# Two graph-attention layers on one core: a head group's value product as one block of matmuls or as four quarters

## What is computed

```python
h = jnp.maximum(_layernorm(x, axis=-1), 0.0)
# layer 0: 8 heads of 32 features
Q, K, V = (proj(Wq, bq), proj(Wk, bk), proj(Wv, bv))
scores = jnp.einsum('bhnd,bhmd->bhnm', Q, K) * SCALE
scores = jnp.where(adj[:, None, :, :] == 0, -jnp.inf, scores)
attn = jax.nn.softmax(scores, axis=-1)
out = jnp.einsum('bhnm,bhmd->bhnd', attn, V)      # the value product
x = x + (out.transpose(0, 2, 1, 3).reshape(b, n, DOUT) @ Wo.T + bo)
# layer 1: edge scores of relu(layernorm(x)), leaky relu, masked softmax, product with the features
```

## Time and profile before

| | |
|---|---|
| median of 3 runs (lowest to highest) | 3978.39 us (3978.27 to 3991.85) |
| span of the profiled execution, first to last instruction | 3976.3 us |
| mean granted TensorE clock over the span | 0.967 of full speed |
| busy share of TensorE matmul / weight load / VectorE / ScalarE / GpSimd | 92% / 73% / 79% / 57% / 17% |

### The profile page before, as it was taken

One profiled execution on the slowest core, in us unless ns is written; L12 is line 12 of the kernel. 1 busy time (PEld: TensorE's weight loads), 2 busy tenths in 40 slices (PEclk: granted clock), 3 DMA queues, 4 the chain that ended last, 5 costly groups with the idle time before them and its releaser, 6 DMA issues.

```text
span 3976.3 us, 94630 instructions
## 1 busy us (share of the span) xinstructions
PE 3669.7 (92%) x34096; PEld 2908.9 (73%) x34096; DVE 3128.6 (79%) x5926; ACT 2267.1 (57%) x3940; POOL 674.9 (17%) x440
## 2 busy tenths in 40 slices
PE   6989989899998989989899898998989989899998
PEld 5777777777777767777777777776777767777776
DVE  6968778687886978869788696886968869688785
ACT  3837547275573845738456384663836638366482
POOL 1021030310303103031020301203012030120300
PEclk8999999999999999999999999999999999999999
DMA  5041220403204032040310503104031040311300
GB/s 151 2 105 36 60 82 2 117 25 70 71 2 118 23 76 66 2 131 10 81 61 4 137 2 83 59 15 126 2 89 53 21 121 2 95 47 31 99 2 12
DMA packets 129070, 227.67 MB, mean 57 GB/s; under 512 B 20672, under 2 KB 71104, under 8 KB 128448
## 3 DMA queue, kind: packets, MB, share of 16 engines
q1 hardware_dynamic: 128448, 219.50, 20.3%
HBM read 101.98 MB, written 16.78 MB: 30 GB/s over the span
## 4 chain that ended last, share of the span: by engine, by line
PE 68%; SPq 11%; issue 9%; DVE 7%; DMA 2%; ACT 1%; DVEq 0%; POOL 0%; POOLq 0%; ACTq 0%
PE pT L856 21%; PE ps L837 15%; PE pO L873 13%; SPq L220 11%; PE ps L773 8%; PE pO L975 7%; PE pT L908 2%; DMA adj_half<-in_adj_dram 2%; PE pT L963 2%; DVE pt L525 1%; DVE most L483 1%; DVE sm L667 1%; PE pO L884 1%; DVE sm L510 1%; DVE sm L674 1%
## 5 line engine op out<-in xcount | busy, mean ns | idle before, releaser
L349 ACT ACTIVATE sm<-sm,mn 128x1024 f32<-128x1024 f32 x1024 | 1179.5, 1152 | 454.8 <-DVE mn L510 452.5
L510 DVE CUSTOM_DVE_ANT_0 sm<-ps,bias 128x1024 f32<-128x1024 f32 x1024 | 1250.9, 1223 | 197.5 <-PE ps L837 178.0
L856 PE MATMUL pT<-ident,sm 128*128 128x128 f32 x8192 | 1098.6, 276 | 40.3 <-DVE pt L525 37.1
L856 PEld LDWEIGHTS pT<-ident,sm 128*128 128x128 f32 x8192 | 961.3, 142 | 218.5 <-DVE pt L525 52.8
L837 PE MATMUL ps<-ks,qs 96*128 96x512 f32 x2048 | 754.4, 451 | 4.6 <-issue 3.7
L525 DVE COPY pt<-pT 128x512 f32<-128x512 f32 x1024 | 702.4, 686 | 31.5 <-PE pT L856 30.8
L873 PE MATMUL pO<-pt,v 128*32 128x128 f32 x16384 | 649.7, 278 | 4.8 <-DVE pt L525 4.8
L359 ACT COPY pt<-pT 128x512 f32<-128x512 f32 x1024 | 583.2, 570 | 56.7 <-PE pT L856 56.4
L290 POOL TENSOR_SCALAR bias<-adj_half 128x512 bf16<-128x512 int32 x240 | 468.0, 1950 | 864.3 <-DMA adj_half<-in_adj_dram 855.7
L873 PEld LDWEIGHTS pO<-pt,v 128*32 128x32 f32 x16384 | 388.2, 109 | 170.1 <-issue 170.1
L975 PE MATMUL pO<-h,pt 128*128 128x256 f32 x2048 | 463.0, 379 | 0.0
(11 more groups left out here) (104 smaller groups left out, 3526.5 us busy)
## 6 DMA issues: line engine op xcount, KB each, us to landing
adj_half<-in_adj_dram SPq DMA_DIRECT2D x256, 256.0 KB, 2.8
ks<-pt SPq DMA_DIRECT2D x384, 128.0 KB, 2.4
qs<-pt SPq DMA_DIRECT2D x384, 128.0 KB, 2.4
xf<-in_x_dram SPq DMA_DIRECT2D x16, 1024.0 KB, 8.0
x<-in_x_dram SPq DMA_DIRECT2D x16, 1024.0 KB, 5.7
out_dram<-x SPq DMA_DIRECT2D x128, 128.0 KB, 2.9
x<-in_L_gnn_Wq_dram SPq DMA_DIRECT2D x1, 256.0 KB, 2.8
x<-in_L_gnn_Wk_dram SPq DMA_DIRECT2D x1, 256.0 KB, 3.1
```

The lines of the kernel that those rows point to most:

```text
L349: nc.scalar.activation(sm[:, t % RING, :], sm[:, t % RING, :], ACT.Exp, scale=-1.0, bias=mn[:, t:t + 1], accum_out=den[:, t:t + 1]).then_i ...
L510: nc.vector.tensor_tensor_reduce(out=sm[:, t % RING, :], in0=ps[t % 2][:, :], in1=bias[:, node, :], scale=1.0, scalar=3e38, op0=ALU.add, o ...
L856: last = nc.tensor.transpose(pT[c][:, j * P:(j + 1) * P], sm[:, t % RING, m * P:(m + 1) * P], ident[:, :])
```

## The change

In layer 0, `values` loses its argument `part`. It now makes all 32 matmuls of a group in one block, directly behind the transposes of the first tile of the next group (t = 4, 8, ..., 60), and signals `av` at the end of that block. In the other three tiles of a group no value matmul stands. The last group's product, after the loop, is the same block as before. No operation is added or removed.

```diff
-                def values(g, part):
+                def values(g):
                     hg, quad = g // NT, g // 4
-                    if part == 0:
-                        pe.wait_ge(pt_made[0], TILES * b + HG * (g + 1))
-                        pe.wait_ge(pt_made[1], TILES * b + HG * (g + 1))
-                    if g % 4 == 0 and quad and part == 0:
+                    pe.wait_ge(pt_made[0], TILES * b + HG * (g + 1))
+                    pe.wait_ge(pt_made[1], TILES * b + HG * (g + 1))
+                    if g % 4 == 0 and quad:
                         pe.wait_ge(r_copied, QUADS * b + quad)
                         pe.wait_ge(normed, QUADS * b + quad - 1)
                     n = slice(g % 4 * P, (g % 4 + 1) * P)
-                    for m in range(NT // 4 * part, NT // 4 * (part + 1)):
+                    for m in range(NT):
                         for h in range(HG):
...
-                    if part == 3:
-                        last.then_inc(av, 1)
+                    last.then_inc(av, 1)
...
-                    if t >= HG:
-                        values(t // HG - 1, t % HG)
+                    if t and t % HG == 0:
+                        values(t // HG - 1)
...
-                for part in range(4):
-                    values(GROUPS - 1, part)
+                values(GROUPS - 1)
```

## The result

The change made the kernel slower: 4107 us (median of 4 runs, 4091 to 4118) against 3981 us (median of 4 runs, 3978 to 3992), a ratio of 1.0317 with a 95% interval of 1.0282 to 1.0351. The forecast was 4115, in 4065 to 4160. The profiled execution has a span of 4089.2 us; it is the fastest of the four.

The account below looks back on a forecast made before the run. TensorE was taken to bound layer 0 before, and afterwards the chain behind the block. 15 graphs at 8.7 us plus 6.8 for the last make 137 us more, giving a 4115 us median; range 4065 to 4160.

Parts of the forecast that it names:

- What bounds layer 0: Kernel before: TensorE sets the group of four tiles at 8.45 us; VectorE and ScalarE need 7.0 us.
- TensorE's saving: Value product in one block of 1.88 us, entered once a group: TensorE's work falls from 8.45 to 7.51 us a group.
- The chain behind the block: Late scores, then masks, copies and transposes up to the next block: 8.81 us a group against 8.45; VectorE idle some 1.75.
- The link to the next transposes: Next group's first tile: second half of its transposes starts 0.73 us after VectorE's last copy began, at 9.18 us.
- Statistics and aggregation: Next graph's VectorE work: four statistics of 0.34 us on the chain, 1.4 us a graph, plus 0.5 for aggregation at tile 30.
- The row block: `rows` after tiles 16, 32, 48: ScalarE's copy waits for the block; 9.40 us block to block, 0.6 us a graph extra.
- End of layer 0: Transposes of tile 60 to those of 63: 6.95 us instead of 5.62, 1.3 us a graph more.
- The sum: All terms of layer 0 together: 8.7 us a graph slower, 6.8 for the last graph, 137 us in all.
- the lower bound: Layer 0 with a group at 8.69 us and aggregation and `rows` free: 5.9 us a graph, 4073 us.
- the rival with a falling clock: TensorE's clock falls in layer 0 because it waits every group: at most 55 us more, 4170 us; chance 4 in 100.
- TensorE as the bound at 7.5: Rival: TensorE still sets layer 0's group at 7.51 us, 225 us less, 3753 us; chance 5 in 100.

Follow-up runs that it names:

- the eighths: Kernel before with each quarter of the value product cut in two, one piece behind each half of a tile's transposes; one run, 4255 us.
- The halves: Changed kernel with the value product in two parts, behind the transposes of a group's first and third tile; 4094 us, 1.026 of the kernel before.
- the scores ahead: Changed kernel, block left whole, only the scores of the group's fourth tile made before it; 4053 us, 1.016 of the kernel before.
- the scores ahead of halves: Value product in two parts, with scores and the row block's transposes made before each; 3888 us, 0.976 of the kernel before.

## Why the prediction was right, step by step

- **What bounds layer 0, and TensorE's saving.** Right. The block is 1.88 us, entries are a quarter, and the eighths priced an entry with its exit at 0.29 us against the 0.31 of the sum.
- **The chain behind the block.** Right to 0.02 us: 8.81 forecast, 8.79 measured; the mask's wait was to be about 1.75 and is 1.74. The halves, forecast by the same links at 8.86 a group and measured at 8.88, and the scores ahead, at 8.35 and measured at 8.35 to 8.45, show that it is this chain and not the length of the block.
- **The link to the next transposes.** Right, though the timeline hides it. The eight transposes at 1356.37 stand in one row there, begun as ScalarE's copy of the tile before lets them, and no stall is printed between their halves. A narrower window on the weight loader shows where the second half begins:

```profile
1356.88 0.31 PEld L856 LDWEIGHTS pT<-ident,sm 128*128 128x128 f32 x3
```

  That is 0.51 us after the first, where the working has 0.44 for four transposes that nothing holds, and 0.75 after VectorE's copy began (1356.13). Two tiles earlier the second half begins 0.74 after VectorE's copy (1352.65), and there the wait is long enough to be printed:

```profile
1353.39 0.66 PE L856 MATMUL pT<-ident,sm 128*128 128x128 f32 x4 [0.28 <-DVE pt L525]
```

  So both copies hold the transposes of the next group's first tile, ScalarE's their first half and VectorE's, which ends last by less than 0.1 us, their second, as the working said (8.70 and 8.74).
- **Statistics and aggregation.** Right. The forecast counted from block to block. The blocks behind the transposes of tiles 20, 24, 28 and 32 are

```profile
1375.45 1.95 PE L872 MATMUL pO<-pt,v 128*32 128x128 f32 x64
...
1384.58 1.95 PE L872 MATMUL pO<-pt,v 128*32 128x128 f32 x64
...
1394.03 1.95 PE L872 MATMUL pO<-pt,v 128*32 128x128 f32 x64
...
1404.20 1.96 PE L872 MATMUL pO<-pt,v 128*32 128x128 f32 x64
```

  with distances of 9.13, 9.45 and 10.17 us: the plain 8.79 with one statistic of 0.34 (tile 22), with two (25 and 26), and with one and the aggregation (29 and 30), 1.04. From first transposes to first transposes the same work shows partly a group later, as two distances that are 0.65 longer than a plain one and 10.29 against 9.25 over a row block alone. The kernel before paid 0.58 of it (9.42 against 8.84), so 0.46; 0.5 was taken. Moving them all into VectorE's idle time won nearly the whole of it back.
- **The row block: mis-sized.** The sum had 9.40 from block to block over tile 16, 0.2 beyond the excess of a plain group. Measured, with TensorE's lines first and ScalarE's behind them:

```profile
1366.27 1.96 PE L872 MATMUL pO<-pt,v 128*32 128x128 f32 x64
...
1375.45 0.75 PE L872 MATMUL pO<-pt,v 128*32 128x128 f32 x20
```

```profile
1369.33 1.15 ACT L349 ACTIVATE sm<-sm,mn 128x1024 f32<-128x1024 f32 x1
...
1370.47 0.57 ACT L359 COPY pt<-pT 128x512 f32<-128x512 f32 x1
1370.94 1.16 ACT L349 ACTIVATE sm<-sm,mn 128x1024 f32<-128x1024 f32 x1
```

  From block to block that is 9.18. ScalarE, when nothing holds it, goes from a copy to the next exp in 0.47 us, not in the 0.60 that was taken from VectorE; the working has two such steps, so its 9.40 is 0.26 too long, and at 9.14 ScalarE no longer ends last: VectorE's chain, a plain group's 8.79 and 0.4 for TensorE's four transposes, gives the 9.18. In the trace the two end within 0.03 us of each other. Against 8.84 before that is 0.34, a plain group's loss, so this term was nothing instead of 0.6 a graph. The 0.49 of the earlier trace rows was the nearer row and was set aside.
- **End of layer 0.** Forecast 6.95 from the transposes of tile 60 to those of 63, measured 7.05 (5.62 before).
- **The sum.** Forecast 8.7 us a graph. Measured over 15 graphs, transposes of tile 4 to those of tile 60 went from 120.45 to 126.91, and with the end that is 6.46 + 1.43 = 7.9; the last graph, without statistics, lost 5.9. 15 x 7.9 + 5.9 = 124 us, and the medians differ by 126 (4107 - 3981). Most of the 13 us between the 124 and the forecast's 137 is the row block's 0.6 x 16. Two slips in the working move nothing: 14 x (8.81 - 8.45) is 5.0 and not 4.9, and the lower bound charges the statistics to the last graph too (4071 instead of 4073).
- **The profiled execution** shows only 113 us, since 0.7 us a graph came back outside tiles 4 to 63. Its mean granted clock is 0.974 against 0.967, so TensorE was at its lower level (0.50) for about 2 x 0.026 x 4089 = 213 us instead of 262, which goes with it but was not tested. How much of it the other runs had is not known, so it may be partly chance that the medians' 126 lies so near to the 124. From tile 4 to tile 60 the granted clock was 1.00 in all 16 graphs, so the rival with a falling clock didn't occur; the lower level lay at the start of layer 0 and outside it.
- **The rivals.** TensorE as the bound at 7.5 needed masks to do during the block; with one such mask (the scores ahead) a whole block still took 8.35, since its next late thing was a copy. A third `ps` or a second `pT`, which the rival also named, wasn't tried. The rule of the Trainium skill, Perfetto Trace Analysis, section Optimization Strategy, that interleaving such regimes may improve performance pointed the right way. The runs add that it isn't the length of the stretch alone but what is queued behind it: halves lost as much as the whole block, and with the scores ahead of them were 2.4% faster than the kernel before.

## What to carry to other kernels

Before making an engine's work cheaper by gathering it, list what stands behind the gathered block in that engine's order and follow it to the next block: if the only work that the other engines could do meanwhile is there, the distance between blocks is that chain, however well the totals fit. Hand out their work first (here one pair of score matmuls ahead of each block), then gather, and gather only as much as that work covers: gathered first, it cost 3.2%; with the scores ahead of the whole block 1.6%; with the scores ahead of halves it won 2.4%. And price an operation by its place: VectorE's statistics and aggregation cost 2.4 us a graph on the chain and next to nothing inside a wait.

## What had not been expected of the hardware

ScalarE begins an exp 0.47 us after a 0.57 us copy began (1370.47 to 1370.94), before that copy's record ends, and so keeps a pace of 1.61 us for exp and copy (1369.33 to 1370.94). VectorE too begins its next mask before the record of its copy ends, but 0.60 us after a 0.69 us copy of the same size began (1300.11 to 1300.71).
